# A mixture of experts inside a fused kernel: the shared expert's last product is made during the experts' stage, and nine of 32 experts are multiplied in fp32

## What is computed

```python
T, D, I, E, K = 1024, 256, 128, 32, 4
C = ceil(1.25 * T / E)                          # 40 places for each expert
topk_idx, topk_w = _router(x, router_w, e_bias)
...                                             # slots_token, slots_w: token and weight of each place
Xp = x[slots_token].reshape(E, C, d)
G = jnp.einsum('ecd,edi->eci', Xp, W_gate)
U = jnp.einsum('ecd,edi->eci', Xp, W_up)
Y = jnp.einsum('eci,eid->ecd', silu(G) * U, W_down)
Yf = Y.reshape(EC, d) * slots_w[:, None]
out = jnp.zeros((T, d)).at[slots_token].add(Yf)
shared = silu(x @ shared_gate.T) * (x @ shared_up.T) @ shared_down.T
return out + shared
```

## Time and profile before

| | |
|---|---|
| median of 3 runs | 1072.01 us (1067.32 to 1075.21) |
| the profiled execution | 1076.02 us, its span 1074.3 us |
| PE busy over the span | 945.2 us (88%) |
| DVE, ACT, POOL | 75%, 59%, 45% |
| mean granted TensorE clock | 0.943 |

### The profile page before, as it was taken

One profiled execution on the slowest core, in us unless ns is written; L12 is line 12 of the kernel. 1 busy time (PEld: TensorE's weight loads), 2 busy tenths in 40 slices (PEclk: granted clock), 3 DMA queues, 4 the chain that ended last, 5 costly groups with the idle time before them and its releaser, 6 DMA issues. The chain is left out here.

```text
span 1074.3 us, 18349 instructions
## 1 busy us (share of the span) xinstructions
PE 945.2 (88%) x6414; PEld 589.3 (55%) x6414; DVE 806.0 (75%) x1445; ACT 630.6 (59%) x1097; POOL 483.1 (45%) x385
## 2 busy tenths in 40 slices
PE   5976977999999999999999998799698699899797
PEld 4455764555555655555655553496243366576334
DVE  3958437999999999999999999255899557454267
ACT  3646037888788888788887887224310257455241
POOL 3130744566765565755566550210582137432263
PEclk9985889999999999999999999899899799999799
DMA  5575115788888889879879879601125167589532
GB/s 172 112 190 168 31 45 91 154 147 179 167 171 168 150 162 179 178 159 167 158 156 183 159 141 215 147 2 60 54 79 161 46 188 220 171 244 281 164 92 84
DMA packets 380882, 155.61 MB, mean 145 GB/s; under 512 B 287557, under 2 KB 378231, under 8 KB 380535
## 3 DMA queue, kind: packets, MB, share of 16 engines
q1 hardware_dynamic: 363286, 131.23, 56.6%
q10 hardware_dynamic: 14432, 14.81, 4.1%
q0 software_dynamic: 3072, 8.39, 2.3%
HBM read 60.93 MB, written 23.72 MB: 79 GB/s over the span
## 5 line engine op out<-in xcount | busy, mean ns | idle before, releaser
L940 DVE SCALAR_TENSOR_TENSOR a_halves<-a_ex,a_share,a_halves 128x1024 f16<-128x1024 f32 x128 | 190.3, 1487 | 36.7 <-ACT a_halves L934 34.7
L1237 DVE TENSOR_REDUCE a_nmax<-psum 128x1 f32<-128x1024 f32 x128 | 156.5, 1223 | 7.1 <-PE psum L1106 6.8
L1026 POOL TENSOR_TENSOR a_rnorm<-a_ss,a_power 128x8 f32<-128x8 f32 x32 | 67.9, 2121 | 194.4 <-DVE a_ss L1213 194.3
L934 ACT ACTIVATE a_halves<-a_ex,a_share 128x1024 f16<-128x1024 f32 x128 | 146.7, 1146 | 12.4 <-DVE a_share L1243 6.5
L1180 ACT ACTIVATE a_ex<-psum,a_nmax 128x1024 f32<-128x1024 f32 x128 | 142.6, 1114 | 0.5 <-DVE a_nmax L1237 0.5
L1088 PE MATMUL psum<-a_wh,xT_h 128*128 128x128 f16 (+1 forms) x512 | 116.1, 249 | 3.7 <-PEq L2659 2.0
L1089 PE MATMUL psum<-a_wl,xT_h 128*128 128x128 f16 (+1 forms) x512 | 116.1, 249 | 0.0
L1090 PE MATMUL psum<-a_wh,xT_l 128*128 128x128 f16 (+1 forms) x512 | 115.9, 249 | 0.0
L1118 PE MATMUL psum<-a_pT,a_vh 128*128 128x512 f16 x256 | 98.2, 384 | 9.9 <-DMA a_pT<-a_halves 9.9
L1119 PE MATMUL psum<-a_pT,a_vh 128*128 128x512 f16 x256 | 98.0, 383 | 0.0
L1120 PE MATMUL psum<-a_pT,a_vl 128*128 128x512 f16 x256 | 98.0, 383 | 0.0
(11 more groups left out here) (389 smaller groups left out, 2408.8 us busy)
## 6 DMA issues: line engine op xcount, KB each, us to landing
block_outputs<-g_e_ym ACTq DMA_DIRECT2D x16, 512.0 KB, 3.4
split_rest<-a_e_wh SPq DMA_DIRECT2D x15, 384.0 KB, 3.1
wf<-in_L_ffn_W_gate SPq DMA_DIRECT2D x32, 128.0 KB, 2.5
wf<-in_L_ffn_W_up SPq DMA_DIRECT2D x32, 128.0 KB, 2.6
wf<-in_L_ffn_W_down SPq DMA_DIRECT2D x32, 128.0 KB, 3.1
g_rows<-sorted_tokens SPq DMA_DIRECT2D x16, 256.0 KB, 4.5
g_e_raw<-in_L_ffn_wg SPq DMA_DIRECT2D x32, 128.0 KB, 3.2
g_e_raw<-in_L_ffn_wu SPq DMA_DIRECT2D x32, 128.0 KB, 3.5
```

What stands on the lines that cost most here:

```text
L934: act.activation(halves[i % PB][:, :, 0, :], ex[m % 2][:, :].rearrange("p (k q) -> p k q", q=P), ACT.Copy, scale=share[:, m:m + 1]).then_i ...
L940: dve.scalar_tensor_tensor(halves[i % PB][:, :, 1, :], ex[m % 2][:, :].rearrange("p (k q) -> p k q", q=P), share[:, m:m + 1], halves[i % P ...
L1237: dve.tensor_reduce(nmax[:, k:k + 1], score_banks(m), AX.X, ALU.max, negate=True).then_inc(max_ready, 1)
```

## The change

Three things. First, the shared expert's last product leaves `combine0`. POOL makes `hT` at the start of `experts0`, PE makes one of the eight tiles in each second round from round 8 to round 22, in one bank (7), and ACT copies it to `gate0` in the round after. In `combine0`, DVE adds the sum to what stands in `gate0`. Second, the experts with e >= 8 and e % 8 in (1, 4, 7), nine of them (9, 12, 15, 17, 20, 23, 25, 28, 31), are not split: PE multiplies fp32 weights with fp32 tokens (`xg_f`, which POOL adds from the two parts) and fp32 hidden values, four products for gate and up and two for down. Third, what this asks for: 17, 20 and 23 are loaded into the memory of `w_h` and `w_l` of their buffer, which is now one tile `whl`; outputs use three banks in turn instead of four; and some waits count splits instead of experts.

```diff
+WHOLE = (1, 4, 7)
+def whole(e):
+    return e >= EB and e % EB in WHOLE
+def expert_buffer(env, e):
+    return env["w_other"][e % EB] if whole(e) and e // EB == 2 else env["wf"][e % EB][:, :, :]
...
+        OUTS, SHARED_BANK = 3, 7
+        def shared_tile(e):
+            n, odd = divmod(e - SHARED_FROM, 2)
+            return n if e >= SHARED_FROM and not odd and n < NT else None
...
                 for e in range(2 * EB, E0):
-                    sp.wait_ge(w_ready, e - EB + 1)
+                    if whole(e):
+                        sp.wait_ge(y_ready, (e - 2 * EB) + 1)
+                    else:
+                        sp.wait_ge(w_ready, splits(e - EB))
                     load_expert(sp, env, e, e % EB)
...
+                def gate_up_whole(i, b):
+                    pe.wait_ge(loaded[b], 48 * (i + 1))
+                    pe.wait_ge(xg_whole, WHOLE.index(b) + 1)
+                    weight, rows = expert_buffer(env, EB * i + b), env["xg_f"][b]
+                    for j in range(2):
+                        out = psum[:, b % BANKS, j * CAP:(j + 1) * CAP]
+                        for c in range(DC):
+                            last = pe.matmul(out, weight[:, DC * j + c, :], rows[:, c, i - 1, :], start=(c == 0), stop=(c == DC - 1))
+                    last.then_inc(gu_ready, 1)
...
+                def shared_down(i, b):
+                    n = shared_tile(EB * i + b)
+                    if n is None:
+                        return
+                    if n == 0:
+                        pe.wait_ge(shared_h, 2 * IC)
+                    if n:
+                        pe.wait_ge(shared_done, n)
+                    for ic in range(IC):
+                        last = pe.matmul(psum[:, SHARED_BANK, 0:D], hT[:, ic, n * P:(n + 1) * P], w3T[2][:, ic, :],
+                                         start=(ic == 0), stop=(ic == IC - 1))
+                    last.then_inc(shared_ready, 1)
-                rounds((3, down, False), (0, gate_up, False))
+                rounds((3, down, False), (0, gate_up, False), (0, shared_down, False))
...
-                rounds((0, silu, False), (3, next_high, True), (0, hidden_high, False))
+                rounds((0, silu, False), (3, next_high, True), (0, hidden_high, False), (1, shared_copy, False))
...
-                    dve.tensor_copy(gate0[:, n, :], psum[:, 4 + n % 2, 0:D]).then_inc(o_done, 1)
+                    dve.tensor_tensor(gate0[:, n, :], psum[:, 4 + n % 2, 0:D], gate0[:, n, :], ALU.add).then_inc(o_done, 1)
```

More of the change, by code:

```diff
@@ L470, in experts0, with out_place, splits, scale @@
             sem("e0_" + s) for s in ("nwh", "gu", "si", "h", "hh", "hl", "y", "yd"))
+        xg_whole = sem("e0_xf")
+        shared_h, shared_ready, shared_done = (sem("e0_" + s) for s in ("sh", "sr", "sd"))
+        gate0, hT, w3T = (env[k] for k in ("gate0", "shared_hT", "shared_wT"))
+        IC, SHARED_FROM = IS // P, 8
+        OUTS, SHARED_BANK = 3, 7
+        def out_place(e):
+            return psum[:, BANKS + e % OUTS, 0:DC * CAP]
+        def shared_tile(e):
+            n, odd = divmod(e - SHARED_FROM, 2)
+            return n if e >= SHARED_FROM and not odd and n < NT else None
+        def splits(e):
+            return sum(not whole(i) for i in range(e + 1))
+        def scale(i, b):
+            return 1.0 if whole(EB * i + b) else 1.0 / WSCALE
         def rounds(*jobs):
@@ L490, in _, with down_whole @@
             def _(pe):
+                def gate_up_whole(i, b):
[7 more added lines that the diff above has]
+                    last.then_inc(gu_ready, 1)
+                def down_whole(i, b):
+                    pe.wait_ge(h_ready, EB * i + b + 1)
+                    if EB * i + b >= OUTS:
+                        pe.wait_ge(y_done, EB * i + b - OUTS + 1)
+                    weight = expert_buffer(env, EB * i + b)
+                    for c in range(DC):
+                        out = out_place(EB * i + b)[:, c * CAP:(c + 1) * CAP]
+                        last = pe.matmul(out, weight[:, 2 * DC + c, :], hf[b % BANKS][:, :], start=True, stop=True)
+                    last.then_inc(y_ready, 1)
                 def gate_up(i, b):
-                    pe.wait_ge(w_ready, EB * i + b + 1)
+                    if whole(EB * i + b):
+                        return gate_up_whole(i, b)
+                    pe.wait_ge(w_ready, splits(EB * i + b))
                     slots = bass.ds((EB * i + b) * CAP, CAP)
@@ L602, in summed @@
                     pe.matmul(out, turned[n][:, s, :], yw_h[:, s, :], start=(s == 0), stop=False)
-                    pe.matmul(out, turned[n][:, s, :], yw_l[:, s, :], start=False, stop=False)
-                def shared_down(n):
-                    for ic in range(IC):
-                        last = pe.matmul(psum[:, 4 + n % 2, 0:D], hT[:, ic, n * P:(n + 1) * P], w3T[2][:, ic, :],
-                                         start=False, stop=(ic == IC - 1))
-                    last.then_inc(o_ready, 1)
+                    last = pe.matmul(out, turned[n][:, s, :], yw_l[:, s, :], start=False, stop=(s == ST - 1))
+                    if s == ST - 1:
+                        last.then_inc(o_ready, 1)
                 turn_rows(0)
```

70 lines of the change are left out of this document (47 added, 23 removed).

## The result

The changed kernel is slower: 1078.72 us, the median of 18 runs (1068.60 to 1091.21), against 1073.18 for the kernel before (18 runs, 1067.32 to 1076.27). The ratio is 1.0050, its 95% interval 1.0029 to 1.0072. I had forecast 1069, that is 3 us less than before; it became 5.5 us more. The profiled execution took 1077.06 us, its span 1075.3.

A forecast was written before the change was run, and what follows sets the result against it. The experts' stage was taken as bound by DVE first, loads in its middle, the combine by PE; +3.7 us in the stage and -7.0 in the combine gave -3.3, so 1069 us against the median 1072.0, range 1061 to 1083.

The forecast's parts named there:

- The combine, -7.0: Combine stage: eight shared-expert tiles of 0.87 us each leave PE's path, tile period about 2.2, together -7.0 us.
- I take no wait (bound 1.7): Start of the experts' stage: POOL's products and additions end at 73.6 to 77, PE wants them at 75.4; no wait.
- the 0.9 that DVE was to save before round 8: Experts' stage before round 8: two rounds without a weight split save DVE about 0.9 us; PE begins round 8 about 75.0.
- I let the clock rise 5.5 us after it: Experts' stage: PE has no idle time from round 8, so its clock goes from half to full 5.5 us later.
- The waits for the bank, 7 x 0.6 = 4.2: Experts' stage: PE waits for ACT's copy of the tile before, 0.6 us for each of seven tiles, 4.2 us.
- The fp32 records: Whole experts on PE: two records per fp32 product, 0.217 us each at half clock and 0.109 at full.
- rival 4: Experts' stage: weight load sets the fp32 record at 0.217 us at either clock; +8 on the end, 1077 us, chance 0.08.
- DVE's relief: Experts' stage: nine of 24 weight splits go, 7.7 us of DVE, real while DVE is the bound.
- The tail, 12.3 us: Twelve last rounds of the experts' stage: middle between an end at 112.8 (1.2 GHz) and 108.0 (2.4 GHz).
- 110.4: Forecast end of the experts' stage in us, +3.7 on today's 106.7.
- my second rival: Experts' stage: fp32 weights and copy waits keep PE at half clock, end after 113.7; 0.27 for +0 to +12.

The follow-up runs named there:

- e5: Changed kernel without POOL's four products of shared gate and up in the experts' stage: median 1082.10 us, ratio 1.0065 to the kernel before.
- e12: Changed kernel with ACT's copy of the shared tile directly behind the silu, nothing else: median 1073.23 us, ratio 0.9994 to the kernel before.
- e2: Changed kernel with the shared product and POOL's products back in the combine, only the nine fp32 experts kept: median 1076.08 us, ratio 1.0028 to the kernel before.
- e1: Changed kernel with all 32 experts split, only the shared product moved into the stage, one bank: median 1070.63 us, ratio 1.0000 to the kernel before.
- e13: Changed kernel with the copy directly behind the silu and fp32 experts 25, 28, 31 split: median 1071.70 us, ratio 0.9998 to the kernel before.
- e9: Changed kernel with all experts split and ACT's copy of the shared tile directly behind the silu: median 1068.70 us, ratio 0.9960 to the kernel before.

## Why the forecast was wrong, step by step

- **The combine, -7.0.** Right: -6.8, a tile period of 2.18, no fp32 record in it, DVE's addition hidden at 0.42.
- **POOL: "I take no wait (bound 1.7)".** This is the first step that failed. PE indeed did not wait for POOL's results. But I priced POOL as a supplier only and not as a neighbour of DVE. I had round 8 begin at about 75.8 on DVE (75.0 on PE); it began at 79.08 (77.31 on PE). 2.7 of these 3.3 us are POOL's four products (e5). Against them stand 0.3 by which the whole stage began earlier. The rest is the 0.9 that DVE was to save before round 8: in e5, without POOL's products, rounds 4 and 7 take 0.76 instead of 1.23, but rounds 0 and 5 take 1.06 and 1.69 instead of 0.62 and 1.24, and from the first `e_hf` to the ninth it is 8.56 us, against 8.62 before. Round 0's part is `xg_f`, under which an `e_hl` still takes 0.64.
- **The clock: "I let the clock rise 5.5 us after it".** The second failure, the largest. Counted from PE's start of round 8, 77.31, as my sum did, the clock rose after 14.1 us, at 91.4, in the other profile after some 23. The premise "in the new order PE has no idle time from round 8" did not hold, because of my own next term: PE idles in the waits for the bank. In e12, without them, the clock rises at 84.6, 7.3 us after PE's start of the round. But the premise would not have been enough either. In e2 PE stands at 5.00 of 5.00 us from 80 to 85 at 0.50 and the clock never rises in the stage, and in e1, where it rose at 79.0, before the first wait, the waits did not take it away. It was late where fp32 experts and waits came together, and absent where the fp32 experts stood alone; what in PE's work decides is open. In my sum 8.6 us more at the half clock are 4.3 us, and rounds 8 to 22 took 5.3 more than the 23.1 that I gave them.
- **The waits for the bank, 7 x 0.6 = 4.2.** As a sum right: 3.9 us, six of them, at PE's weight loads. As a term of a sum wrong: opening the ring gave back 5.1 us of the stage, since beside the fp32 experts the waits also come with a later clock (3.2 of the 5.1) and, at the full clock, make DVE wait in its turn (the ring of e1; 1.9).
- **The fp32 records.** Their prices hold. With 40 columns, at the half and at the full clock:

```profile
86.56 1.91 PE L533 MATMUL psum<-xg_f,wf 128*128 128x40 f32 x8
88.26 2.05 PE L587 MATMUL psum<-shared_wT,shared_hT 128*128 128x256 f32 x4
...
95.30 1.13 PE L587 MATMUL psum<-shared_wT,shared_hT 128*128 128x256 f32 x4
...
96.42 1.06 PE L533 MATMUL psum<-xg_f,whl 128*128 128x40 f32 x8
97.32 0.62 PE L543 MATMUL psum<-e_hf,wf 128*128 128x40 f32 x4
```

  Eight records take 1.70 us to the next start at 0.50 (0.213 each) and 0.90 at 1.00 (0.113 each), against my 0.217 and 0.109. That clears away rival 4. The Trainium skill, TensorE: Matmul & The Clock Gate, section LDWEIGHTS, gives a weight load as its columns over 1.2 GHz, for 128 columns 0.107 us, with no term for the clock. The records at 1.00 (0.113) are near that figure and those at 0.50 (0.213) near twice it, so if the load sets the pace of so short a record, which no run shows by itself, the runs disagree with it as a rule for both clocks; nor does it give the 0.217 of rival 4.
- **DVE's relief.** I said it was real "while DVE is the bound". It came to nothing: before round 8 it was taken back (above), e13 against e9 and e2 against before lose 3.0 and 1.6 us in rounds 8 to 24, and the last rounds lose 3.2 to 3.5. The most that it gave anywhere is the 0.35 us of e12's rounds 13 to 24.
- **The tail, 12.3 us.** Near in size: 11.6 from DVE's `e_hf` of round 23 (107.45 to 119.0), 13.3 from PE's start of it (105.75). By its parts it was a middle between two clocks, and the clock was at 1.00 up to 111.9 and at 0.50 behind it.

The stage ended at 119.0, not at 110.4. Counted on PE, as the sum was, it is 2.3 at the start, 5.3 in rounds 8 to 22 and 1.0 in the tail, together 8.6. What came is my second rival in the main (the half clock, held by the fp32 weights and the waits for the copy, decided by an end after 113.7), to which I had given 0.27; not in full, since the clock was at 1.00 from 91.4 to 111.9. It was named with its cause; I weighed it too low because I treated waits and clock as two terms that add. That 1078.72 lies inside the range of 1061 to 1083 is no merit of the mechanism: the range was wide, and the sign was wrong.

Open is why the medians of e5 and e1 stand several us from what their stages say, what decides, between two executions alike in the stage up to 92.4 us, whether the clock rises, and why an unbroken row of fp32 products at 40 columns and fp16 ones (e2) did not bring it up.

## What to carry over

Work moved under another stage has to be followed in every in-order queue that it enters: here one copy at the wrong end of ACT's round closed a ring over PE, ACT and DVE, and cost 4 of the 7 us that the combine gained; set directly behind the silu it cost little but itself. In this kernel a wait on PE below the full clock was paid twice, once as time and once as a clock that rose later. And taking work from the busiest engine pays only in rounds where that engine sets the pace, so ask for each round: nine fp32 experts bought room on DVE with PE time that the half clock doubles.

## What the runs showed of the hardware

- POOL operations between SBUF tiles hold up DVE's operations on two SBUF inputs, also short ones: 40 columns took 0.81 to 1.25 us instead of 0.19, 768 columns 1.95 instead of 0.94, and POOL's own two products 3.20 instead of 2.49. DVE's operations that read PSUM kept their time.
- An fp32 product with 40 columns runs as two records of 0.213 us each at a granted 0.50 and 0.113 at 1.00, the paces of 32 columns (0.213 to 0.217) and 128 (0.11 to 0.13). The profile prints 1.00 for the stretch with 32 columns, where the pace is that of 0.50; nothing here settles which of the two is right.
- Two executions of one kernel, alike within 0.1 us in the stage up to 92.4 us, got the full clock 9 us apart (91.4 and 100.1); between the two times lies a wait of PE of 0.8 us.
- With fp32 experts and no shared tile (e2), PE was busy for all of 80 to 85 and 95 to 100 at a granted 0.50, and the clock did not rise before 115.5; with shared tiles and no fp32 expert (e1) it rose at 79.0 and stood at 1.00 from 80 to 100 through waits of 1.0 us in every second round.
